# First relation pass of a graph kernel: TensorE picks the rows of every sixth tile from x on the chip, GpSimd gathers the others

## The chip, the cores and the metric

One core of a Trainium2 chip. The metric is the device time of one execution in microseconds (us). The engines: TensorE (PE; PEld is its weight load), VectorE (DVE), ScalarE (ACT), GpSimd (POOL) and SyncE (SP), which here only issues DMAs and passes semaphores on. In the profile "adj" is one large SBUF tensor that most buffers of the relation passes are carved from, so many tiles show under this name; "banks" is PSUM.

## The reference, cut to what matters

A stack of four graph layers over x (3125 nodes x 128) with 100,000 edges, sorted by destination; each layer is added to x and normalized. The last one is a two-layer relational convolution with 8 relations (128 to 256 to 128 features):

```python
def rgcn_layer(x, src, dst, etype, W, W_root, b, num_rels):
    h = jnp.einsum('ni,rio->rno', x, W)
    msg = h[etype, src]
    seg = dst * num_rels + etype
    sums = segment_sum(msg, seg, N * num_rels)
    cnt = segment_sum(ones, seg, N * num_rels)
    mean = sums / maximum(cnt, 1.0)[:, None]
    return mean.reshape(N, num_rels, do).sum(axis=1) + x @ W_root + b
h = relu(rgcn_layer(x, src, dst, etype, W1, root1, b1, 8))
out = rgcn_layer(h, src, dst, etype, W2, root2, b2, 8)
```

## The kernel before, in words

The edges are cut into T = 782 tiles of 128 edges, the nodes into 196 windows of 16. As the edges are sorted, a walk over JA = 977 steps meets each pair of tile and window that share an edge; most tiles take one step, some two. All of x, split in a high and a low f16 part (256 columns, "split"), also stands in HBM as table1.

At the start (until 66 us) the kernel works the walk out on the chip. VectorE turns the three edge lists into f16 pieces (line 1079 and after); ScalarE and VectorE make one-hot blocks "pick" that say which tile belongs to which step, in two batches (512 and 465 steps) of seven blocks; TensorE multiplies them with the pieces (L479, six matmuls per block); `expand` on VectorE (from L1131) turns the result into codes, windows and tile numbers, which SP stores in HBM. ScalarE begins with the queue of the parameter loads. Until 402 us the adjacency matrix is built from one-hot blocks (L1224 and L1232 on VectorE, L500 on TensorE, L856 on ScalarE), and until 890 us the first three layers run densely on TensorE.

Then come two relation passes with the matmuls of the two layers between (1874 to 2061 us). In a pass:

- GpSimd (`gather`, L766) fetches for each tile its 128 rows of 256 f16 from the table with one indirect DMA into one of NG = 16 buffers of `gath`; from the 17th on it first waits for `slot_free`.
- SP (`relay`, from L405) walks over the tiles in order: it waits until the last step of an old tile is scattered (L411, L412), frees its buffer (`slot_free`, L413 to L416), waits for the landing of tile t and raises `landed`. A buffer is freed eight tiles ahead of the landing that follows.
- VectorE (`relation_sums`, L1521) makes the one-hot block of step j + 4 (L1519, 128x128 f16), and adds the PSUM result of step j to the sums of its window (L1534, 128x129 f32).
- TensorE (`scatter`, L604) waits for the one-hot block, the tile and a free PSUM bank (six), and multiplies twice (L618: 129 and 128 columns). The buffer is chosen by a register, tile number modulo NG.
- ScalarE does nothing in a pass; in the first 83 steps it prepares weights, with pieces of this work on VectorE and TensorE (`between`).

Before the first pass GpSimd waits for the end of the dense layers, writes the ones column of `gath`, small constants and zeros over the sums (L753 to L757), then waits for table1.

## Time and profile before

| | us |
|---|---|
| median of 3 runs | 3111.7 (3109.05 to 3114.53) |
| profiled execution | 3108.86, span 3107.0 |
| walk and adjacency matrix | 0 to 402 |
| dense layers | 402 to 890 |
| first relation pass | 891 to 1874 |
| matmuls between the passes | 1874 to 2061 |
| second relation pass and end | 2062 to 3107 |

The page of the profile in 40 slices (each digit is the busy share in tenths, PEclk the granted clock of TensorE; the passes are the stretches with 7 on POOL):

```profile
PE   4777789989825444444444448964444444444447
DVE  6999949894156444444444445654444444444445
ACT  3555511111120000000000004520000000000003
POOL 0000000000157777777777771147777777777772
PEclk8888889999955555555555558975555555555558
```

A row of a timeline gives the start, the duration, engine, line, operation and tiles, and in brackets the idle time of the engine before it and what ended it. An engine may start an instruction before the duration of the last one has run out, so the distance of two starts is what an instruction costs in a full queue.

### The profile page before, as it was taken

The numbers are of one execution on the slowest core, as the hardware profiler recorded it, in microseconds if no ns is written. First come the engines' busy times: TensorE is split into PE (matmuls) and PEld (weight loads), VectorE is DVE, ScalarE is ACT, GpSimd is POOL, SyncE is SP. The second block draws the span as 40 slices with busy tenths as digits, with TensorE's granted clock in tenths as the row PEclk, the third lists the DMA queues.
The fourth block names the chain that finished last, engine by engine and source line by source line (L and its number), as shares of the span: only waits on it lengthen the run. The fifth ranks groups of instructions, "written<-read, shape, count | busy, mean of one in ns | idle before, by whom it ended". The sixth has DMA issues, their size and how long they took to land.

```text
span 3107.0 us, 50653 instructions
## 1 busy us (share of the span) xinstructions
PE 1742.9 (56%) x10220; PEld 961.0 (31%) x10220; DVE 1782.6 (57%) x6482; ACT 409.4 (13%) x868; POOL 1548.2 (50%) x1653
## 2 busy tenths in 40 slices
PE   4777789989825444444444448964444444444447
PEld 2333354544412222222222227742222222222227
DVE  6999949894156444444444445654444444444445
ACT  3555511111120000000000004520000000000003
POOL 0000000000157777777777771147777777777772
PEclk8888889999955555555555558975555555555558
DMA  2545510080112122222222221122222222222221
GB/s 63 128 117 117 124 42 1 1 263 2 48 49 54 53 54 54 54 54 53 54 53 54 54 54 52 76 71 53 53 54 54 54 53 53 54 53 54 53 54 29
DMA packets 174994, 191.72 MB, mean 62 GB/s; under 512 B 110509, under 2 KB 140990, under 8 KB 174723
## 3 DMA queue, kind: packets, MB, share of 16 engines
q0 software_dynamic: 50048, 102.60, 12.6%
q1 hardware_dynamic: 120774, 84.33, 9.8%
q8 instruction: 124, 2.03, 0.3%
q10 hardware_dynamic: 3900, 1.55, 0.2%
q14 instruction: 148, 1.20, 0.1%
HBM read 130.57 MB, written 38.14 MB: 54 GB/s over the span
## 4 chain that ended last, share of the span: by engine, by line
POOL 40%; PE 17%; DVE 15%; issue 15%; DMA 7%; SPq 3%; ACT 2%; ACTq 1%; DVEq 0%; POOLq 0%
POOL adj L766 40%; DVE hi_hot L1224 6%; DMA adj<-table,adj 6%; PE banks L528 4%; PE banks L543 4%; PE banks L662 3%; SPq L411 2%; DVE lo_hot L1232 2%; PE banks L674 2%; DVE deg_in L1392 2%; PE banks L714 2%; ACTq L848 1%; PE banks L647 1%; DVE stats L1280 1%; PE banks L506 1%
## 5 line engine op out<-in xcount | busy, mean ns | idle before, releaser
L766 POOL DMA_INDIRECT adj<-table,adj x1564 | 1478.6, 945 | 511.5 <-issue 454.4
L618 PE MATMUL banks<-adj 128*128 x3908 | 807.8, 286 | 1173.6 <-DVE adj L1519 778.1
L1534 DVE TENSOR_TENSOR adj<-adj,banks 128x129 f32 x1954 | 565.9, 290 | 1002.4 <-PE banks L618 919.5
L618 PEld LDWEIGHTS banks<-adj 128*128 128x128 f16 x3908 | 408.3, 105 | 1578.1 <-issue 1533.0
L1519 DVE TENSOR_SCALAR adj<-adj 128x128 f16<-128x128 f16 x1954 | 548.6, 281 | 1.5
L500 PE MATMUL banks<-hi_hot,lo_hot 128*128 128x400 f16 x977 | 248.1, 383 | 100.8 <-DVE hi_hot L1224 60.3
L1224 DVE TENSOR_SCALAR hi_hot<-iota,zT 128x400 f16<-128x400 f16 x977 | 250.9, 315 | 21.3 <-PE banks L500 21.2
L543 PE MATMUL banks<-adj,split 128*128 128x512 f16 (+1 forms) x1078 | 217.1, 359 | 0.0
L753 POOL MEMSET adj<- 128x32 f16 x1 | 0.1, 128 | 422.9 <-PE banks L543 422.9
L750 POOL PARTITION_ALL_REDUCE small<-small x1 | 0.4, 380 | 406.1 <-DVE small L1324 406.1
L500 PEld LDWEIGHTS banks<-hi_hot,lo_hot 128*128 128x128 f16 x977 | 114.9, 118 | 234.5 <-issue 172.7
L528 PE MATMUL banks<-adj,split 128*128 128x512 f16 (+1 forms) x672 | 138.9, 371 | 24.6 <-DVE adj L1419 13.6
L1046 ACT ACTIVATE adj<-adj 128x128 f32<-128x128 f32 x75 | 22.0, 387 | 987.0 <-DVE adj L1545 987.0
L1005 ACT ACTIVATE adj<-banks 128x512 f16<-128x512 f32 x50 | 26.9, 585 | 899.0 <-PE banks L647 899.0
L543 PEld LDWEIGHTS banks<-adj,split 128*128 128x128 f16 x1078 | 100.0, 99 | 108.2 <-issue 6.9
L856 ACT ACTIVATE adj<-banks 128x400 f16<-128x400 f32 x196 | 97.9, 501 | 158.9 <-PE banks L500 133.4
L1232 DVE TENSOR_TENSOR lo_hot<-iota,zT 128x512 f16<-128x512 f16 (+1 forms) x245 | 101.4, 415 | 0.0
L777 POOL MEMSET adj<- 128x1032 f32 x25 | 23.9, 957 | 154.5 <-PE banks L647 154.5
L528 PEld LDWEIGHTS banks<-adj,split 128*128 128x128 f16 x672 | 63.8, 101 | 98.9 <-issue 24.8
L860 ACT ACTIVATE banks<-banks 128x400 f32<-128x400 f32 x188 | 91.7, 488 | 6.0
L1392 DVE TENSOR_REDUCE deg_in<-adj 128x1 f32<-128x3200 f16 x25 | 85.1, 3475 | 0.0
L662 PE MATMUL banks<-adj,w1p 128*128 128x128 f16 x1350 | 84.2, 221 | 1.0 <-ACT h L1015 1.0
(241 smaller groups left out, 1280.7 us busy)
## 6 DMA issues: line engine op xcount, KB each, us to landing
adj<-table,adj POOLq DMA_INDIRECT x1564, 2.5
adj_copy<-adj SPq DMA_DIRECT2D x24, 800.0 KB, 3.9
adj<-adj_copy SPq DMA_DIRECT2D x6, 2176.0 KB, 15.8
table<-adj SPq DMA_DIRECT2D x25, 512.0 KB, 2.6
adj<-adj_copy SPq DMA_DIRECT2D x1, 3072.0 KB, 10.4
adj<-adj_copy SPq DMA_DIRECT2D x3, 1024.0 KB, 15.3
table<-split SPq DMA_DIRECT2D x6, 256.0 KB, 2.3
out_dram<-xres SPq DMA_DIRECT2D x6, 256.0 KB
```

Of the source, the lines that this page charges most:

```text
L500: e.matmul(banks[:, bass.ds(c, 1), 0:NC].rearrange("p o n -> p (o n)"), low, hi_hot[:, j % NHI, :], start=False, stop=True, skip_group_che ...
L528: m = e.matmul(sums_of(a, c), split[:, k, s, :], sources(a, k, c), start=(k == 0 and s == 0), stop=False)
L543: m = e.matmul(sums_of(a, c), split[:, k, s, :], sources(a, k, c), start=False, stop=(k == NB - 1 and s == 1))
L618: m = e.matmul(bank[j % NSUM][:, 0:b - a], hot[:, j % NHOT, :], edge[:, a:b], start=(q == 0), stop=(q == 1), skip_group_check=True)
L662: m = e.matmul(bank[3][:, o * P:o * P + P], w1p[:, wq, r, o * P:o * P + P], rowT[:, s, zq, r, :], start=(i == 0 and r == 0), stop=(i == 2 ...
L766: e.indirect_dma_start(gath[:, (t + 1) % NG, 0:2 * D], None, table, bass.IndirectOffsetOnAxis(ap=index[:, which, t:t + 1].bitcast(U32), ax ...
L856: e.activation(blocks[:, min(g + 1, LASTG), :, at * WA:(at + 1) * WA], v.rearrange("p (h n) -> p h n", n=WA), ACT.Copy).then_inc(evicted, 1)
L1224: e.tensor_scalar(hi_hot[:, j % NHI, :], iota[:, :], code[:, j:j + 1], None, ALU.is_equal).then_inc(high, 1)
L1232: e.tensor_tensor(lo_hot[:, g % NLO, :, 0:n], iota4[:, :, 0:n], lo[:, k:k + n].unsqueeze(1).broadcast_to([P, P, n]), ALU.is_equal).then_in ...
L1392: e.tensor_reduce(deg_in[:, b:b + 1], adj[:, b, :], AX.X, ALU.add).then_inc(in_degrees, 1)
L1519: e.tensor_scalar(hot[:, s, :], iota_r[:, :], code_r[:, j:j + 1], None, ALU.is_equal).then_inc(hot_set, 1)
L1534: e.tensor_tensor(a, a, bank[j % NSUM][:, 0:D + 1], ALU.add).then_inc(accumulated, 1)
```

## The change

In the first pass every sixth tile from tile 120 on (120, 126, ... 780: 111 tiles) is no longer gathered. Its rows are picked from `split`, which is now kept in SBUF through the pass (`place`, `hTp` and `h32` take its space afterwards). The source numbers of a picked tile, less 0, 640, ... 2560, were stored in HBM as f16 at the start (`scr_s`, by six GpSimd operations over 128x896 and one SP store). ScalarE's queue loads the five rows of a tile, broadcast to all partitions (`source_row`, 164 KB, two in flight). VectorE compares each row with a constant block of 5 x 128 node numbers (`select_hots`, one comparison of 128x640 f16 per step in five of six steps, steps 111 to 775), TensorE multiplies the five 128x128 blocks that come out with five blocks of `split` (`select_part`, 5 matmuls of 256 columns per step, steps 114 to 778), summing 25 in bank 6 or 7, and ScalarE copies the sum to one of NGX = 34 further buffers of `gath`. TensorE waits for that copy one step after the step without a part.

GpSimd gathers the other 671 tiles into NG = 18 buffers. SP raises `landed` for a picked tile without a wait. The buffer of a tile no longer follows from its number alone: buffer number times 1024 is added to the tile number in the walk. For this GpSimd makes a row of buffer numbers, stores it in HBM and loads it back by columns, VectorE copies it to a seventh piece before the others, each pick has a seventh matmul, and `expand` casts the word and masks the tile number out. In the second pass all tiles are gathered, into 18 buffers. The ones columns of the late buffers, which lie over w2, are written by VectorE at step 115; GpSimd's zeros over the sums move ahead of the ones block, and the ones block and the new constant wait for the last dense matmuls. The core of the diff:

```diff
+    KB = 5
+    PARTS = NB // KB
+    NG, NGX = 18, 34
+    by_pe = range(FROM, T, EVERY)
+    NPE = len(by_pe)
+    by_gather = [t for t in range(T) if t not in by_pe]
+    ROUND = EVERY * NGX
+    BUFS = FROM + -(-(TB * P - FROM) // ROUND) * ROUND
...
-        SUMS_OF = {0: [S_LO], 1: [S_HI, TYPE], 2: [D_LO, D_HI], 3: [TILE]}
+        SUMS_OF = {0: [S_LO], 1: [S_HI, TYPE], 2: [D_LO, D_HI], 3: [TILE, BUF]}
...
+            e.wait_ge(source_set, 1 + PARTS)
+            e.dma_start(scr_s, source16.rearrange("p b k e -> p b (k e)")).then_inc(source_out, 16)
...
+                block = None
                 for t in range(T):
                     u = t + LEAD - NG
-                    if u >= 0 and t + LEAD < T:
-                        if u % REGS == 0:
-                            n = min(REGS, T - NG - u)
-                            e.load(last_regs[0:n], last_row[:, u:u + n])
+                    if u >= 0 and u + NG in tiles_of(which):
+                        if u // REGS != block:
+                            block = u // REGS
+                            n = min(REGS, T - block * REGS)
+                            e.load(last_regs[0:n], last_row[:, block * REGS:block * REGS + n])
                         e.reg_alu(least, last_regs[u % REGS], 1, ALU.max)
                         if which:
                             e.reg_alu(least, least, JA, ALU.add)
                         e.wait_ge(scattered, least)
                         e.sem_inc(slot_free[which], 1)
-                    e.wait_ge(gathered[t % NG], 16 * (which * (-(-(T - t % NG) // NG)) + t // NG + 1))
+                    if t in tiles_of(which):
+                        e.wait_ge(gathered[t % NG], 16 * landings(which, t))
                     e.sem_inc(landed[which], 1)
...
+            def select_part(j):
+                i, q = divmod(j - FROM + EVERY, EVERY)
+                if q == 0 and 0 < i <= NPE:
+                    e.wait_ge(copied, i)
+                if q < PARTS and 0 <= i < NPE:
+                    e.wait_ge(selected, PARTS * i + q + 1)
+                    if q == 0 and i >= 2:
+                        e.wait_ge(copied, i - 1)
+                    for k in range(q * KB, (q + 1) * KB):
+                        m = e.matmul(bank[6 + i % 2][:, 0:2 * D], select[:, k, :], split[:, k, :, :].rearrange("p s d -> p (s d)"),
+                                     start=(k == 0), stop=(k == NB - 1), skip_group_check=True)
+                    m.then_inc(part_summed, 1)
+
             def scatter(which):
                 base = which * JA
                 for j in range(JA):
                     if j % WORDS == 0:
                         n = min(WORDS, JA - j)
                         e.load(tile_regs[0:n], tile_row[:, j:j + n])
-                    e.reg_alu(least, tile_regs[j % WORDS], 1, ALU.max)
+                    if which == 0:
+                        select_part(j)
+                    e.reg_alu(least, tile_regs[j % WORDS], (1 << BUF_LOG2) - 1, ALU.bitwise_and)
+                    e.reg_alu(least, least, 1, ALU.max)
                     e.wait_ge(hot_set, base + j + 1)
                     e.wait_ge(landed[which], least)
-                    c = e.snap(tile_regs[j % WORDS], min_val=1, max_val=T) % NG
+                    if which:
+                        c = e.snap(least, min_val=1, max_val=T) % NG
+                    else:
+                        word = e.snap(tile_regs[j % WORDS], min_val=1, max_val=((NG + NGX) << BUF_LOG2) - 1)
+                        c = word // (1 << BUF_LOG2)
...
+            e.iota(buf_row[:, :], pattern=[[0, BUFS // NG], [1 << BUF_LOG2, NG]], base=0, channel_multiplier=0,
+                   allow_small_or_imprecise_dtypes=True).then_inc(own_pool, 1)
+            e.wait_ge(own_pool, 1)
+            late = buf_row[:, FROM:BUFS].rearrange("a (c i s) -> a c i s", i=NGX, s=EVERY)[:, :, :, 0]
+            e.iota(late, pattern=[[0, (BUFS - FROM) // ROUND], [1 << BUF_LOG2, NGX]], base=NG << BUF_LOG2, channel_multiplier=0,
+                   allow_small_or_imprecise_dtypes=True).then_inc(own_pool, 1)
+            e.wait_ge(own_pool, 2)
+            e.dma_start(scr_b.rearrange("(a n) -> a n", a=1), buf_row[:, :]).then_inc(buffers_out, 16)
+            e.wait_ge(buffers_out, 16)
+            e.dma_start(buf_col[:, :], scr_b[0:TB * P].rearrange("(b q) -> q b", q=P),
+                        allow_slow_non_contiguous=True).then_inc(buffers_in, 16)
...
+            e.wait_ge(pieces_set, 1)
+            e.tensor_tensor(source[:, :, :], piece[:, S_LO, :, :], piece[:, S_HI, :, :], ALU.add).then_inc(source_set, 1)
+            e.wait_ge(source_set, 1)
+            for q in range(PARTS):
+                e.tensor_scalar(source16[:, :, q, :], source[:, :, :], -float(q * KB * P), None, ALU.add).then_inc(source_set, 1)
...
-            e.memset(gath[:, :, 2 * D:2 * D + 2], 1.0).then_inc(rel_set, 1)
+            e.memset(gath[:, 0:NEARLY, 2 * D:2 * D + 2], 1.0).then_inc(rel_set, 1)
             e.iota(iota_r[:, :], pattern=[[1, P]], base=0, channel_multiplier=0,
                    allow_small_or_imprecise_dtypes=True).then_inc(rel_set, 1)
+            e.memset(sums[:, :, :], 0.0).then_inc(sums_zero, 1)
+            e.wait_ge(mlp_sum, 2 * NCH)
             e.memset(ones_all[:, :], 1.0).then_inc(ones_set, 1)
-            e.memset(sums[:, :, :], 0.0).then_inc(sums_zero, 1)
+            e.iota(blocks5[:, :, :], pattern=[[P, KB], [0, P]], base=0, channel_multiplier=1,
+                   allow_small_or_imprecise_dtypes=True).then_inc(blocks5_set, 1)
...
-                for t in range(T):
-                    s = t % NG
+                for t in tiles_of(which):
                     if t >= NG:
-                        e.wait_ge(slot_free[which], t - NG + 1)
+                        e.wait_ge(slot_free[which], released[which].index(t) + 1)
                     e.indirect_dma_start(
-                        gath[:, (t + 1) % NG, 0:2 * D], None, table,
-                        bass.IndirectOffsetOnAxis(ap=index[:, which, t:t + 1].bitcast(U32), axis=0)).then_inc(gathered[s], 16)
+                        gath[:, (t + which) % NG, 0:2 * D], None, table,
+                        bass.IndirectOffsetOnAxis(ap=index[:, which, t:t + 1].bitcast(U32), axis=0)).then_inc(gathered[t % NG], 16)
 
             e.wait_ge(list_in, 80)
...
+            e.wait_ge(source_out, 16)
...
+            def source_row(i):
+                b, p = divmod(by_pe[i], P)
+                e.dma_start(source_rows[:, i % 2, :, :].rearrange("p k e -> p (k e)"),
+                            scr_s[p:p + 1, b, :].broadcast_to([P, PARTS * P])).then_inc(source_in[i % 2], 16)
+
+            for i in range(2):
+                source_row(i)
...
+            e.wait_ge(late_ones, 1)
+            for i in range(NPE):
+                e.wait_ge(part_summed, PARTS * (i + 1))
+                if i >= NGX:
+                    e.wait_ge(scattered, by_pe[i - NGX] + JA - T + 1)
+                e.activation(gath[:, NG + i % NGX, 0:2 * D], bank[6 + i % 2][:, 0:2 * D], ACT.Copy).then_inc(copied, 1)
+                if i + 2 < NPE:
+                    source_row(i + 2)
...
+            e.wait_ge(buffers_in, 16)
+            e.tensor_copy(piece[:, BUF, :, :], buf_col[:, :].unsqueeze(2).broadcast_to([P, TB, P])).then_inc(own_dve, 1)
...
-                e.scalar_tensor_tensor(out=WIN, in0=sets[3][:, 0:n], scalar=-1.0, in1=st, op0=ALU.mult,
-                                       op1=ALU.add).then_inc(own_dve, 1)
-                at_win = own.up()
+                e.tensor_copy(WORD, sets[3][:, 0:n]).then_inc(own_dve, 1)
+                at_word = own.up()
...
+                e.wait_ge(own_dve, at_word)
+                e.tensor_scalar(AT, WORD, (1 << BUF_LOG2) - 1, None, ALU.bitwise_and).then_inc(own_dve, 1)
...
+                e.wait_ge(own_dve, at_at)
+                e.tensor_tensor(WIN, st, AT, ALU.subtract).then_inc(own_dve, 1)
...
+            def select_hots(j):
+                i, q = divmod(j - FROM + EVERY + EVERY // 2, EVERY)
+                if q < PARTS and 0 <= i < NPE:
+                    if q == 0:
+                        e.wait_ge(source_in[i % 2], 16 * (i // 2 + 1))
+                    if i:
+                        e.wait_ge(part_summed, PARTS * (i - 1) + q + 1)
+                    e.tensor_tensor(select[:, q * KB:(q + 1) * KB, :],
+                                    source_rows[:, i % 2, q, :].unsqueeze(1).broadcast_to([P, KB, P]),
+                                    blocks5[:, :, :], ALU.is_equal).then_inc(selected, 1)
...
+                    if which == 0:
+                        select_hots(j)
...
+                elif t == 56 + RR + HB * RR:
+                    e.wait_ge(w_low, RR + HB * RR)
+                    e.memset(gath[:, NEARLY:NG + NGX, 2 * D:2 * D + 2], 1.0).then_inc(late_ones, 1)
```

## Rows read from the trace of the kernel before

**Rows 1.** The page: chain by engine; costliest group (busy, mean ns | idle before); DMA landing

```profile
POOL 40%; PE 17%; DVE 15%; issue 15%; DMA 7%; SPq 3%; ACT 2%; ACTq 1%; DVEq 0%; POOLq 0%
...
L766 POOL DMA_INDIRECT adj<-table,adj x1564 | 1478.6, 945 | 511.5 <-issue 454.4
...
adj<-table,adj POOLq DMA_INDIRECT x1564, 2.5
```

**Rows 2.** Busy time by stretch, the clock after the engines

```profile
core 0: us, PE busy (x) PEld busy (x) DVE busy (x) ACT busy (x) POOL busy (x), PEclk, DMA share, GB/s
66.00:400.00 334.00, 246.76 (x974) 114.31 (x972) 309.62 (x1209) 178.12 (x380) 0.00 (x0) 0.90 0.51 118
1200.00:1850.00 650.00, 268.40 (x1298) 135.46 (x1298) 315.12 (x1297) 0.00 (x0) 491.53 (x521) 0.50 0.20 54
1890.00:2050.00 160.00, 160.00 (x1833) 126.93 (x1832) 105.24 (x183) 82.77 (x183) 24.83 (x35) 1.00 0.18 74
```

**Rows 3.** Waits in 1200 to 1850: us in total, times, longest us

```profile
DVE adj L1534 <- PE banks L618: 304.6, 408, 2.8
...
POOL adj L766 <- issue: 152.7, 501, 0.3
...
POOL adj L766 <- SPq L416: 6.1, 20, 0.3
```

**Rows 4.** Timeline of GpSimd: first and last gather of the first pass

```profile
890.87 1.30 POOL L766 DMA_INDIRECT adj<-table,adj  x1 [23.24 <-DMA table<-split]
...
1867.03 0.94 POOL L766 DMA_INDIRECT adj<-table,adj  x1 [0.30 <-issue]
```

**Rows 5.** Timeline where work has piled up after a late landing

```profile
1504.40 0.29 DVE L1534 TENSOR_TENSOR adj<-adj,banks 128x129 f32 x1 [1.94 <-PE banks L618]
1504.60 0.25 DVE L1519 TENSOR_SCALAR adj<-adj 128x128 f16<-128x128 f16 x1
...
1504.72 0.41 PE L618 MATMUL banks<-adj 128*128 x2 [1.01 <-DVE adj L1534]
1504.91 0.29 DVE L1534 TENSOR_TENSOR adj<-adj,banks 128x129 f32 x1
...
1505.31 0.41 PE L618 MATMUL banks<-adj 128*128 x2 [0.18 <-DVE adj L1534]
```

**Rows 6.** Timelines of VectorE: f16 comparisons in the adjacency stage and before the pass

```profile
201.14 0.42 DVE L1232 TENSOR_TENSOR lo_hot<-iota,zT 128x512 f16<-128x512 f16 x1
...
201.48 1.02 DVE L1224 TENSOR_SCALAR hi_hot<-iota,zT 128x400 f16<-128x400 f16 x4
...
888.29 0.73 DVE L1519 TENSOR_SCALAR adj<-adj 128x128 f16<-128x128 f16 x4
```

**Rows 7.** TensorE in the chain: 112 matmuls of 512 columns, 12 of 465

```profile
420.85 24.27 PE banks L528 x112
...
44.45 4.96 PE banks L479 x12
```

**Rows 8.** Timelines: VectorE and GpSimd at the same time

```profile
898.74 0.94 POOL L766 DMA_INDIRECT adj<-table,adj  x1 [0.30 <-issue]
...
899.25 0.45 DVE L1519 TENSOR_SCALAR adj<-adj 128x128 f16<-128x128 f16 x1
...
2059.08 3.49 DVE L1692 TENSOR_TENSOR zT<-zT,xres 128x3200 f32<-128x3200 f32 x1
...
2061.67 1.77 POOL L766 DMA_INDIRECT adj<-table,adj  x1 [12.22 <-DMA table<-adj]
```

**Rows 9.** Timelines: start of the kernel, and GpSimd before the first pass

```profile
2.31 0.54 POOL L727 TENSOR_SCALAR adj<-ident 128x128 f16<-128x128 f32 x1
...
9.35 1.08 DVE L1079 CAST adj<-adj 128x896 f16<-128x896 f32 x1
...
21.84 1.33 ACT L828 ACTIVATE adj<-adj 128x512 f16<-128x512 f16 x2
...
846.03 21.60 POOL L757 MEMSET adj<- 128x25800 f32 x1
```

More of the change, by code:

```diff
@@ L19 @@
 GATES, ENDS = 8, 8
+EVERY, FROM = 6, 120
+BUF_LOG2 = 10
 WORDS = 8
@@ L777, in _ @@
                 e.memset(sums[:, nb * WPG:(nb + 1) * WPG, :], 0.0).then_inc(sums_zero, 1)
-            e.memset(place[:, :, :], 0.0).then_inc(own_pool, 1)
+            e.memset(place, 0.0).then_inc(own_pool, 1)
             half = ident[:, :]
```

71 lines of the change are left out of this document (52 added, 19 removed).

## The prediction

> **What bounds the kernel now.** First the shares: GpSimd is 40% of the chain that ended last, the largest part, and all but all its work is line 766, the gathers [rows 1]. Then the stretches: in 1200 to 1850 us GpSimd is busy 491.5 of 650 us, VectorE 315, TensorE 268 at a granted clock of 0.50, ScalarE nothing [rows 2]. The waits of the same stretch say that VectorE waits for TensorE, 304.6 us in 408 waits, while GpSimd has only 0.3 us ahead of each gather, 501 times "issue" and 20 times the release of a buffer by SP, and that is no longer than the others [rows 3]. So the relation passes go at GpSimd's own pace. The timeline prices that pace: the first gather of the first pass starts at 890.87, the last, the 782nd, at 1867.03, so (1867.03 - 890.87) / 781 = 1.250 us each, 0.944 of it busy and 0.30 between two [rows 1, 4]. The pass has 977 steps (one step is one tile with one window of 16 nodes), thus 1.00 us per step. What else a step needs is less: where work has piled up, VectorE does a step in 0.51 us (accumulate at 1504.40 and 1504.91) and TensorE in 0.59 us (1504.72, 1505.31) at half clock [rows 5].
>
> **What is removed.** 111 of 782 gathers (tiles 120, 126, ... 780) leave GpSimd: 111 x 1.250 = 139 us. The remaining 671 cost 671 x 1.250 = 839 us: the floor of the pass. A gather that is left out takes its wait, index read and DMA of 128 rows with it, all in this 1.250. That the gain is full needs VectorE, TensorE and the ring to follow at 0.8 x 1.250 x 5/6 = 0.83 us per step.
>
> **What VectorE gets.** In 665 steps (114 to 778, five of each six) one comparison of 128x640 f16 is added. Nearest row: the comparison of line 1232, also with a broadcast operand, 128x512 f16; the next instruction starts 0.34 us after it [rows 6]. By elements above some 0.07 fixed that is 0.40 us. A loaded step is accumulate 0.20 [rows 5], one-hot 0.16 to 0.31 (four in a row take 0.73 with 0.25 for the last, so 0.16 from start to start; 0.31 to the next accumulate, with register work that the new operation would now cover) [rows 5, 6], and 0.40: 0.76 to 0.91, and I take 0.86, with some 0.1 for waits at the port (below). With the sixth step at 0.51: (5 x 0.86 + 0.51) / 6 = 0.80 us per step, just under 0.83. If the comparison ran at half that pace, it would be 0.73. The comparison waits for its source row and for TensorE's part of the picked tile before, three steps back in TensorE's order; behind that wait stand all further accumulates, but TensorE is ahead of VectorE in any step: 0, unless TensorE is late itself (next).
>
> **What TensorE gets.** Five matmuls of 256 columns in each of these steps. 112 of 512 columns took 24.27 us at full clock, 0.217 each, so 0.11 us for 256; 12 of 465 at half clock took 4.96 us, 0.41 each, so 0.23 for 256 [rows 7]. Five: 0.54 or 1.14 us. The scatter's own step of 0.59 is 0.23 of loads and matmuls and 0.36 of waits and register work [rows 5], which its sequencer can do beneath queued matmuls, at best all of it. A loaded step is then 0.65 to 1.0 us at full clock and 1.37 to 1.73 at half; with the sixth step, 0.64 to 0.93 and 1.24 to 1.54. Here the granted clock decides. Now TensorE waits most of the time and has 0.50 (1.2 GHz). In 66 to 400 us, with 974 matmuls of 400 columns in 334 us (1.17 columns per ns), the clock was 0.90, thus four fifths of that time at 2.4 GHz; when it worked without a pause, 1890 to 2050, it was 1.00 [rows 2]. The changed stretch would have 25 x 256 + 6 x 257 = 7942 columns in six steps, 1.5 per ns at 0.87 us a step. At half clock it would not pause at all. I take four fifths at full clock: 0.8 / 0.80 + 0.2 / 1.3 = 1.15 steps per us, 0.87 us per step.
>
> **Ring and end.** The ring has 18 buffers, so gathers run at most 18 tiles ahead. When step 778 ends (about tile 624), tiles after 642 are still to fetch: 140 x 5/6 = 117 gathers, 146 us. The side of the steps is 114 x 1.00 + 665 x 0.87 + 146 + 4 for the last landing = 843 us, the gather side 839. As long as a step stays under about 0.87, gathers decide; each 0.01 us above adds 6.7 us.
>
> **The shared port.** First the rows. The one-hot of 899.25 fell into the gather of 898.74, took 0.45 instead of 0.25 us and ended with it, while those that start early in a gather take 0.25: GpSimd keeps VectorE off for a part of each gather. And the first gather of the second pass started at 2061.67 while an addition of two SBUF tensors, 2059.08 to 2062.57, ran; it took 1.77 instead of 0.94 us [rows 8]. That is the form of the new comparison: two SBUF inputs. In the first pass no such operation runs: the accumulate reads PSUM, the one-hot has one tensor. If a gather has to wait only where its start falls into a comparison, that is 5 x 0.33 of each 5.2 us, a chance of 0.32 with 0.17 us left on average: 0.05 us, for the some 445 gathers of the stretch 24 us. Bounds: 0 (the two fall into step and miss each other) and the whole 0.40 for each (178 us). I take 27 us. The Trainium skill (SBUF — State Buffer, Who interferes with whom) says that a VectorE instruction with two SBUF inputs contends with a GpSimd instruction that reads SBUF, and that the second to issue blocks until the first ends; it infers that descriptor generation needs only the write side. By the inference the loss would be 0 and the sum 27 us less; the trace's 1.77 us agrees with the block.
>
> **ScalarE, SP, DMA.** 111 copies of 128x256 (two of 128x512 take 1.33 [rows 9], so under 0.67 each) and 111 broadcast loads of 164 KB from HBM, queued behind them, lie on an engine that has nothing to do there [rows 2]; a load has some eight steps, 7 us, and a gather lands in 2.5 us [rows 1], so nothing of it shows. TensorE waits for the copy of a tile one free step after its last part; queued behind that wait is the scatter, with three steps in hand over VectorE: 0. The relay on SP passes over the picked tiles. The ones column of the late buffers is one small memset on VectorE at step 115, under 1 us. Before the pass GpSimd now does ones and block numbers after its 21.6 us of zeros, which end at 867.6, and has until the table is out at 890.87, 23 us of idle time [rows 4, 9]: 0. The second pass has two more buffers and one more register operation; its pace is GpSimd's: 0.
>
> **Start.** VectorE's copy of buffer numbers (1.08 like line 1079) waits for an HBM round trip on GpSimd's queue: two iotas after 4 us, some 1 to 2 us, a store of one row, 2.5 to land like a gather, and 896 pieces of 4 bytes, at most 896/128 x 0.94 = 6.6 us to issue, 2.5 to land: ready at 10 to 18 us, VectorE being ready for it at 10.4. It has some 4 us in hand, for the first pick waits for ScalarE, which has its queue of parameter loads and two copies ahead and begins at 21.84 [rows 1, 9]: 0 to 4, I take 1. A matmul more in each of 14 picks: 7 x 0.22 + 2 x 0.41 on the chain = 2.4. Per batch of 512 or 465 columns a cast and a mask more, at most 1.2 ns per column like line 1079 [rows 9]: 1.2 to 2.4, I take 1.9. GpSimd's six new passes over 128x896 can keep VectorE off its port (0.54 for 128x128 [rows 9], so up to 3 us each): 0 to 10, I take 1. The SP store of the picked rows' sources waits on them, ahead of the plan's stores, and ScalarE's first eviction at 66 waits for its landing: covered unless GpSimd is later than about 50. Behind GpSimd's own round trip stand its iotas and gates, which nobody needs before 60: 0. In all +6 (4 to 15).
>
> **Sum.** Against the profiled execution's 3108.9 us (span 3107.0; the median of three is 2.8 higher): gathers -139, port +27, steps that lag a little behind at low clock and at the change of pace +10, start +6, odds +2: -94, so 3015, and 3018 beside the median.
>
> **The rivals.**
> - Steps near 1.0 us per step: waits between engines or more time at half clock. 114 + 665 + 150 = 929 in place of 978, and +8 for start and odds: 3068. For it: VectorE and TensorE come within a few per cent of the pace. Against: 18 buffers smooth it.
> - TensorE stays at half clock, because it also waits for VectorE. 1.24 per step: 114 + 825 + 150 = 1089, +111 + 8: 3228; at 1.54 200 more. It decides from 1.06 us per step. Against: columns and clock of [rows 2].
> - The port, on the slower side: each gather of the stretch is held up by a whole comparison, 0.40 us: 839 + 178 = 1017, +39 + 8: 3156. It decides from 139 / 445 = 0.31 us per gather. The rule of the Trainium skill, SBUF — State Buffer, Who interferes with whom, would bring this about if a gather read SBUF throughout. Against: a one-hot early in a gather isn't delayed [rows 8].
> - The comparison runs at half pace, 0.73: (5 x 1.19 + 0.51) / 6 = 1.08 per step, 114 + 718 + 150 = 982, +4 + 8: 3121.
> - It doesn't do what it says: the time of the removed gathers returns as waits for landing or buffers: 3117.
>
> **How the numbers follow.** Forecast 0.53 (own range 2975 to 3045), steps near 1.0 0.24 (3045 to 3100), half clock 0.08, port 0.08, half pace 0.04, no effect 0.03. The lower end is the full 139 with a start of 4: 2974, and some less, 2970; the upper one takes in the second case: 3100. A measurement tells 0.2%, 6 us, from no change. Faster 0.80 (the first two and a little of the others), same 0.03, slower 0.17.
>
> **What would show it.** 671 gathers of the first pass, its last start near 1770; if start to start stays 1.25 in the stretch, the port is free, at 1.30 or more it isn't. The comparison at about 0.48 busy, next start 0.40 after. The clock of 1010 to 1600 near 0.9. GpSimd waiting for SP's release there would mean that the steps decide. The first eviction near 72 us. Wrong makes it a clock near 0.5 in the stretch, a comparison of 0.7, or gathers of 1.3 us busy.

## The result and the profile after

| | before | after |
|---|---|---|
| median, same chip | 3110.64 us (4 runs) | 3026.88 us (4 runs, 3025.28 to 3027.63) |
| profiled execution | 3108.86, span 3107.0 | 3026.34, span 3024.5 |
| first eviction of the walk's result | 66.22 | 86.51 |
| first relation pass, first to last gather start | 890.87 to 1867.03 | 913.15 to 1782.98 |
| second pass, first to last gather start | 2061.67 to 3038.28 | 1977.34 to 2955.32 |

The change makes the kernel 2.7% faster: the ratio is 0.9727 (95% interval 0.9715 to 0.9739), 84 us. The prediction said 3018 us with a range of 2970 to 3100, so it holds, and it promised 9 us too much. By the gathers' starts the first pass got 106.3 us shorter (976.2 to 869.8), while 22.3 us were lost ahead of it (first gather 890.87 to 913.15), and the second pass grew by 1.4 us (976.6 to 978.0).

The page of after: the 40 slices, the shares of the chain, and the lines that answer to [rows 1] and show the new work (after the bar: busy us, mean ns of one; then the idle us before them and what ended it).

```profile
PE   3677779998954578888886459944444444444447
DVE  5999977895344688888886556644444444444445
ACT  1555531111130000000000015500000000000003
POOL 3000000000037777777777751167777777777772
PEclk9888879999975699999997569955555555555558
...
POOL 34%; PE 20%; DVE 18%; issue 14%; DMA 10%; SPq 2%; ACT 1%; ACTq 1%; DVEq 0%; POOLq 0%
...
L850 POOL DMA_INDIRECT adj<-table,adj x1453 | 1407.4, 969 | 479.0 <-issue 399.0
...
L659 PE MATMUL banks<-split,zT 128*128 128x256 f16 x2775 | 397.1, 275 | 50.3 <-DVE zT L1638 35.0
...
L1638 DVE TENSOR_TENSOR zT<-zT,blocks 128x640 f16<-128x640 f16 x555 | 268.8, 484 | 0.0
...
L1095 ACT ACTIVATE adj<-banks 128x256 f16<-128x256 f32 x111 | 42.7, 385 | 579.0 <-PE banks L659 574.3
```

There are 1453 gathers where there were 1564, so 111 are gone. One is 0.969 us on average and was 0.945: this is the first trace of the port. In the slices of the stretch with picked tiles (15 to 21) VectorE is at 8 and TensorE at 7 or 8 where both were at 4, GpSimd still at 7, and the granted clock is 9 where it was 5. ScalarE's 111 copies take 0.385 us each, and it waits 574.3 us for TensorE ahead of them; TensorE in turn waits for them 0.3 us in the whole of 1050 to 1550.

By stretch (columns as in [rows 2]), with two more stretches of the pass and one of the second pass:

```profile
1010.00:1400.00 390.00, 308.88 (x2558) 216.64 (x2558) 314.98 (x1216) 25.96 (x68) 299.77 (x297) 0.96 0.32 80
1400.00:1590.00 190.00, 158.73 (x1363) 113.14 (x1364) 161.46 (x626) 14.03 (x37) 145.80 (x146) 1.00 0.35 84
1590.00:1775.00 185.00, 101.35 (x594) 56.65 (x592) 114.02 (x470) 2.69 (x7) 140.49 (x147) 0.60 0.22 58
2000.00:2900.00 900.00, 368.56 (x1800) 187.08 (x1800) 427.11 (x1798) 0.00 (x0) 680.75 (x720) 0.50 0.21 54
```

TensorE, now busy for 79 and 84% of the time, was granted 0.96 and then 1.00, that is 2.4 GHz nearly throughout; in the second pass, where little changed for it (one register operation more, 18 buffers in place of 16), it stayed at 0.50. VectorE is busy 81 to 85% of the changed stretch, and still GpSimd decides, as its waits in 1050 to 1550 show (compare [rows 3]):

```profile
DVE adj L1655 <- PE banks L684: 72.3, 133, 2.1
...
POOL adj L850 <- issue: 91.5, 300, 0.3
...
POOL adj L850 <- SPq L461: 24.4, 80, 0.3
```

No gather of this stretch, nor of the whole first pass, had more than 0.32 us ahead of it, whether "issue" or SP's release ended it. VectorE waits 72.3 us for TensorE in 500, where it waited 304.6 in 650. The steps have come close to the gathers' pace, but not past it.

### The profile page after: what moved, and what is told of

Read it like the earlier page. It is cut to its first block, busy times and chain, and to the rows that moved or that the text cites. A ratio compares the mean times of both kernels' runs of the same rounds, so it can differ in the third digit from the quotient of the medians.

```text
span 3024.5 us, 58937 instructions
## 1 busy us (share of the span) xinstructions
PE 1951.6 (65%) x13009; PEld 1166.5 (39%) x13009; DVE 1943.0 (64%) x7043; ACT 452.9 (15%) x979; POOL 1496.3 (49%) x1553
## 3 DMA queue, kind: packets, MB, share of 16 engines
q14 instruction: 153, 1.25, 0.1%
## 4 chain that ended last, share of the span: by engine, by line
POOL 34%; PE 20%; DVE 18%; issue 14%; DMA 10%; SPq 2%; ACT 1%; ACTq 1%; DVEq 0%; POOLq 0%
POOL adj L850 33%; DMA adj<-table,adj 9%; DVE hi_hot L1334 7%; PE banks L574 4%; PE banks L589 4%; PE banks L728 3%; DVE lo_hot L1342 2%; PE banks L740 2%; SPq L456 2%; DVE deg_in L1502 2%; PE banks L659 2%; PE banks L780 2%; PE banks L684 1%; PE banks L713 1%; ACTq L933 1%
## 5 line engine op out<-in xcount | busy, mean ns | idle before, releaser
L850 POOL DMA_INDIRECT adj<-table,adj x1453 | 1407.4, 969 | 479.0 <-issue 399.0
L684 PE MATMUL banks<-adj,hot 128*128 x3908 | 757.0, 265 | 815.1 <-DVE hot L1629 352.5
L684 PEld LDWEIGHTS banks<-adj,hot 128*128 128x128 f16 x3908 | 396.2, 101 | 1186.6 <-issue 1094.2
L1629 DVE TENSOR_SCALAR hot<-adj 128x128 f16<-128x128 f16 x1954 | 523.3, 268 | 1.5
L659 PE MATMUL banks<-split,zT 128*128 128x256 f16 x2775 | 397.1, 275 | 50.3 <-DVE zT L1638 35.0
L659 PEld LDWEIGHTS banks<-split,zT 128*128 128x128 f16 x2775 | 244.4, 98 | 84.4 <-issue 38.7
L1638 DVE TENSOR_TENSOR zT<-zT,blocks 128x640 f16<-128x640 f16 x555 | 268.8, 484 | 0.0
L1095 ACT ACTIVATE adj<-banks 128x256 f16<-128x256 f32 x111 | 42.7, 385 | 579.0 <-PE banks L659 574.3
## 6 DMA issues: line engine op xcount, KB each, us to landing
adj<-adj_copy SPq DMA_DIRECT2D x1, 3072.0 KB, 10.4
```

Source lines behind the costliest of these rows:

```text
L659: m = e.matmul(bank[6 + i % 2][:, 0:2 * D], select[:, k, :], split[:, k, :, :].rearrange("p s d -> p (s d)"), start=(k == 0), stop=(k == N ...
L684: m = e.matmul(bank[j % NSUM][:, 0:b - a], hot[:, j % NHOT, :], edge[:, a:b], start=(q == 0), stop=(q == 1), skip_group_check=True)
L850: e.indirect_dma_start(gath[:, (t + which) % NG, 0:2 * D], None, table, bass.IndirectOffsetOnAxis(ap=index[:, which, t:t + 1].bitcast(U32) ...
L1629: e.tensor_scalar(hot[:, s, :], iota_r[:, :], code_r[:, j:j + 1], None, ALU.is_equal).then_inc(hot_set, 1)
L1638: e.tensor_tensor(select[:, q * KB:(q + 1) * KB, :], source_rows[:, i % 2, q, :].unsqueeze(1).broadcast_to([P, KB, P]), blocks5[:, :, :], ...
```

## Experiments

The first four ran on the same chip as the kernels before and after, beside 11 further runs of the kernel before (median 3110.29).

### Is the pass shorter by the gathers, and is the start a price of its own?

**three_tiles** picks only tiles 768, 774 and 780 on TensorE. All that prepares for picking at the start stays.

```diff
-EVERY, FROM = 6, 120
+EVERY, FROM = 6, 768
```

> The changed kernel with the picked tiles starting at 768 in place of 120, so three tiles are picked and 779 gathered, while everything that the change adds at the start stays. Theory (the start costs 22 us whatever is picked, and the pass gains by the number of gathers): 3108.9 + 22 - 4 = 3127 us, first gather near 913 us as in the changed kernel, pass 1 at 974 us from first to last gather. Rival (part of the 22 us belongs to the picking of 111 tiles): under 3115 us and a first gather before 905.

Measured: 3129.38 us, ratio to before 1.0061 (1.0038 to 1.0084), so 0.6% slower than before; 3127 had been expected. Its gathers:

```profile
913.37 1.19 POOL L850 DMA_INDIRECT adj<-table,adj  x1 [24.22 <-DMA table<-split]
...
1886.48 0.95 POOL L850 DMA_INDIRECT adj<-table,adj  x1 [0.30 <-issue]
```

The first gather comes where it does in after (913.15), 22 us late, though next to nothing is picked; the pass of 779 gathers takes 973.1 us, 1.25 us each with 0.946 busy. So the loss at the start does not depend on the picking: the kernel is 19.1 us slower than before, and with the 3 x 1.25 us of its own missing gathers that makes 22.8 for the preparation.

### Do the comparisons slow the gathers down?

**no_compare** leaves out the comparisons of line 1638 after those for the first picked tile (the further picked tiles then use its blocks); all matmuls, copies and source rows stay.

```diff
                     if i:
                         e.wait_ge(part_summed, PARTS * (i - 1) + q + 1)
+                    if i:
+                        e.sem_inc(selected, 1)
+                        return
                     e.tensor_tensor(select[:, q * KB:(q + 1) * KB, :],
```

> The changed kernel without the comparisons of VectorE after the first picked tile: TensorE multiplies stale blocks, so 110 tiles get wrong rows; loads, matmuls and copies stay. Theory (the comparison with two SBUF inputs holds gathers up): gathers of the stretch fall from 1.01 to 0.945 us busy, from 1.32 to 1.25 from start to start, the pass from 870 to 843 us, in all near 3000 us. Rival (the row loads or the matmuls do it): gathers stay at 1.01 us and the time at 3026.

Measured: 2995.18 us (two runs, 2991.75 and 2998.62), 31.7 us below after; near 3000 had been expected. The first row here is the group of gathers in 1050 to 1550 of after, the second that of no_compare (busy, mean ns, idle before):

```profile
L850 POOL DMA_INDIRECT adj<-table,adj x380 | 384.9, 1013 | 115.8 <-issue 91.5 <-SPq L461 24.4
```

```profile
L850 POOL DMA_INDIRECT adj<-table,adj x401 | 379.2, 946 | 122.2 <-issue 105.1 <-SPq L461 17.1
```

Without the comparisons a gather takes 0.946 us as in before, with them 1.013; the 0.30 us between two are the same. The pass runs from these two gathers:

```profile
912.10 1.19 POOL L850 DMA_INDIRECT adj<-table,adj  x1 [24.35 <-DMA table<-split]
...
1750.50 0.94 POOL L850 DMA_INDIRECT adj<-table,adj  x1 [0.30 <-issue]
```

That is 838.4 us, the floor of 839 that the prediction worked out for 671 gathers. After needs 869.8, so the comparisons cost 31.4 us. 31.3 us of it is in the durations of the gathers (666.5 us in all against 635.2), 0.1 us in the time between them. The matmuls and the DMAs are the same in both, so of the change's new work it is the comparisons that gathers suffer from. This run alone doesn't say whether by the port or by VectorE's time.

### Is it the port, or VectorE's time?

Two kernels add to the kernel before what the change adds on VectorE, and nothing else: one comparison in 555 steps (five of each six), behind the step's accumulate, with a result that nobody reads (one memset at step 110 fills the inputs first). In **extra_two_sbuf** both inputs are in SBUF (128x640 f16), in **extra_one_sbuf** one is in PSUM (128x320 f32). The same lines stand in both, but for the comparison itself: each kernel has the one under its name (the comments are not in the kernels).

```diff
+            spin = zT[:, 0:4 * 320].rearrange("p (k n) -> p k n", n=320)
+            spin16 = zT[:, 0:4 * 320].bitcast(F16).rearrange("p (k n) -> p k n", n=640)
...
+                    if which == 0 and j == 110:
+                        e.memset(zT[:, 0:4 * 320], 1.0).then_inc(spin_set, 1)
...
+                    if which == 0 and 111 <= j < 777 and (j - 111) % 6 < 5:
+                        e.wait_ge(spin_set, spun.n)
+                        # extra_two_sbuf:
+                        e.tensor_tensor(spin16[:, 0, :], spin16[:, 1, :], spin16[:, 2, :], ALU.is_equal).then_inc(spin_set, 1)
+                        # extra_one_sbuf:
+                        e.tensor_tensor(spin[:, 0, :], bank[7][:, 0:320], spin[:, 2, :], ALU.is_equal).then_inc(spin_set, 1)
```

> The kernel before with one comparison of 128x640 f16 with two SBUF inputs added to steps 111 to 776 (five of six), whose result nobody reads. VectorE has 0.51 us of work in a 1.00 us step, so 0.40 more has room. Theory (port): the 532 gathers of that stretch take 1.01 to 1.02 us and start 1.31 to 1.32 us apart: 532 x 0.07 = 37 us, near 3147 us. Rival (row loads or matmuls slow the gathers, not VectorE): 0.945 us, 1.25 us and 3110 us.

> The kernel before with one comparison of 128x320 f32 in the same steps, one input from PSUM and one from SBUF, which takes VectorE as long as the 128x640 f16 one (about 0.40 us). Theory (only a second SBUF input takes the side that gathers need): gathers stay at 0.945 us, 3110 us. Rival (any VectorE work or any write of it slows them): as with two SBUF inputs, near 3147 us.

Measured: 3132.64 us for two SBUF inputs, ratio 1.0072 (1.0049 to 1.0095); 3109.95 us for one, ratio 0.9998 (0.9987 to 1.0009). The gathers of 1050 to 1600, first with two, then with one:

```profile
L767 POOL DMA_INDIRECT adj<-table,adj x428 | 420.9, 983 | 130.4 <-issue 115.2 <-SPq L417 15.2
```

```profile
L767 POOL DMA_INDIRECT adj<-table,adj x441 | 416.9, 945 | 134.4 <-issue 128.0 <-SPq L417 6.4
```

And a pair of rows of each timeline, a comparison and the gather that starts into it:

```profile
1299.70 0.48 DVE L1549 TENSOR_TENSOR zT<-zT 128x640 f16<-128x640 f16 x1
...
1299.89 1.11 POOL L767 DMA_INDIRECT adj<-table,adj  x1 [0.30 <-issue]
```

```profile
1305.68 0.48 DVE L1549 TENSOR_TENSOR zT<-banks,zT 128x320 f32<-128x320 f32 x1
...
1305.90 0.95 POOL L767 DMA_INDIRECT adj<-table,adj  x1 [0.30 <-SPq L417]
```

Both comparisons keep VectorE busy for 0.48 us. The gather that starts 0.19 us after the first one's start takes 1.11 us, the one 0.22 us after the second one's start 0.95. So it isn't VectorE's time, it is the second SBUF input. The two comparisons also differ in type, f16 against f32, and no run varies that alone. But two f32 inputs in SBUF hold a gather up as well: the first gather of the second pass, which starts into such an addition [rows 8], takes 1.75 to 1.77 us in every trace here, while the first gather of the first pass, with nothing on VectorE beside it, takes 1.19 to 1.30. And the f16 one-hots with one SBUF input, one in each step of the kernel before, leave its gathers at 0.945. The size was missed: 1.01 to 1.02 us busy, 1.31 from start to start and a time of 3147 had been expected, and the runs gave 0.983, 1.288 and 3132.6, about half to two thirds of it. Sorted by where the gather starts after the comparison's start, gathers of extra_two_sbuf take

| gather starts after the comparison's start | its duration |
|---|---|
| 0.05 to 0.10 us | 1.20 to 1.25 |
| 0.15 to 0.20 us | 1.10 to 1.15 |
| 0.20 to 0.25 us | 1.05 to 1.10 |
| 0.30 to 0.35 us | 0.95 to 1.00 |
| 0.35 us and later, into the comparison | 0.945 |

A delayed gather is longer by the rest of the comparison less some 0.125 us: this difference is 0.12 to 0.13 us for nine of ten of them, in extra_two_sbuf and in after. So a comparison that ends within 0.125 us of the gather's start costs nothing. Nor does one that begins 0.15 us or more into a gather: all but one of the 200 gathers of extra_two_sbuf into which one began 0.15 to 0.48 us after their start took 0.94 to 0.95 us. Of the 530 gathers of its stretch 151 started in the first 0.35 us of a comparison (0.28); in after it was 170 of 448 (0.38), and its mean is higher for that. How the two engines fall into step sets the size, and the expectation had taken the share of after for both. The comparison itself takes 0.48 us whatever the phase.

The Trainium skill (SBUF — State Buffer, Who interferes with whom) says that a VectorE instruction with two SBUF inputs contends with a GpSimd instruction that reads SBUF; the trace agrees (1.11 against 0.95). The page infers besides that the generation of a DMA's descriptors needs only the write side, and so isn't held up by such an instruction. Most of a gather fits that; its start doesn't run free, and whether it is the read of its 128 row numbers from SBUF that is held up there was not tried.

### What does the start consist of?

The trace of after, GpSimd's first 41 us (lines 817 and 820 work out the sources):

```profile
4.22 2.21 POOL L801 IOTA adj<- 1x936 f32 x1
...
7.18 0.79 POOL L808 DMA_DIRECT2D scr_buffer<-adj  x1 [0.31 <-POOL adj L805]
18.08 1.04 POOL L810 DMA_DIRECT2D adj<-scr_buffer  x1 [10.12 <-DMA scr_buffer<-adj]
...
25.83 1.92 POOL L817 TENSOR_TENSOR adj<-adj 128x896 f32<-128x896 f16 x1 [5.04 <-DVEq L1199]
27.84 12.92 POOL L820 TENSOR_SCALAR adj<-adj 128x896 f16<-128x896 f32 x5
```

and VectorE's:

```profile
22.27 1.09 DVE L1184 CAST adj<-adj 128x896 f16<-128x896 f32 x1 [12.19 <-DMA adj<-scr_buffer]
...
26.03 1.74 DVE L1202 TENSOR_TENSOR adj<-adj 128x7 f32<-128x7 int32 x1
```

The same operation in both_again (below), which has nothing on GpSimd at that time:

```profile
14.13 0.17 DVE L1215 TENSOR_TENSOR adj<-adj 128x7 f32<-128x7 int32 x1
```

The store of 3.7 KB landed 10.6 us after its issue, the load behind it 4.2 us after its own, and VectorE stood still for 12.19 us, until 22.27; 12.19 us earlier it had been ready for this cast, at 10.1 (the prediction had 10.4). Then GpSimd's passes over the sources took 1.92 + 12.92 us, and VectorE's operation on 128x7 numbers beside the first of them took 1.74 us where it takes 0.17 alone. Two causes, then: the round trip, and the source passes, which hold VectorE up. Four kernels take them away.

**buffers_on_chip** computes the buffer numbers on VectorE, with 15 small operations on 128x7 numbers, and has no round trip:

```diff
-            e.dma_start(scr_b.rearrange("(a n) -> a n", a=1), buf_row[:, :]).then_inc(buffers_out, 16)
-            e.wait_ge(buffers_out, 16)
-            e.dma_start(buf_col[:, :], scr_b[0:TB * P].rearrange("(b q) -> q b", q=P),
-                        allow_slow_non_contiguous=True).then_inc(buffers_in, 16)
...
+            dve(e.scalar_tensor_tensor(out=R18, in0=X[0], scalar=-18.0, in1=tile, op0=ALU.mult, op1=ALU.add))
...
+            e.wait_ge(own_dve, dve(e.tensor_tensor(buf_col[:, :], LB, R18, ALU.add)))
```

> The changed kernel with the buffer numbers worked out by 15 small VectorE operations (128x7 and 128x14) in the time in which it waits for the edge lists, without GpSimd's row, its store and its load. Theory (the round trip keeps VectorE waiting from 10.1 to 22.3 us, of which ScalarE's queue had covered 4 or less): the first eviction comes 10 to 12 us earlier, at 75 to 77 us, in all 3015 us. Rival (the extra matmuls and expand operations are what counts): no more than 3 us.

**sources_by_act** lets ScalarE write the five tables of sources, from the integers that were loaded, and takes GpSimd's six passes out:

```diff
-            e.tensor_tensor(source[:, :, :], piece[:, S_LO, :, :], piece[:, S_HI, :, :], ALU.add).then_inc(source_set, 1)
-            e.wait_ge(source_set, 1)
-            for q in range(PARTS):
-                e.tensor_scalar(source16[:, :, q, :], source[:, :, :], -float(q * KB * P), None, ALU.add).then_inc(source_set, 1)
...
+            for q in range(PARTS):
+                e.activation(source16[:, :, q, :], tab_i[:, 0, :, :], ACT.Copy, bias=-float(q * KB * P)).then_inc(source_set, 1)
```

> The changed kernel with the five blocks of source numbers made by ScalarE from the edge list after its picks (5 x 0.8 us in its idle time) in place of GpSimd's six operations (14.9 us busy). Theory (GpSimd holds the shared port, so VectorE's operations between 26 and 40 us take longer, 1.74 in place of 0.17 for a small one): 5 us less, 3021 us. Rival (hidden): within 2 us of 3026.

**both_and_later** is the two together, and it issues the first two source-row loads behind the wait for the table:

```diff
+            e.wait_ge(l3_in, 16 * (3 + HB))
+            e.wait_ge(table1_out, 16 * NQ)
             for i in range(2):
                 source_row(i)
-            e.wait_ge(l3_in, 16 * (3 + HB))
-            e.wait_ge(table1_out, 16 * NQ)
```

> Both of these, and the first two row loads of ScalarE's queue moved behind the landing of the table (they were issued 0.4 us before the last store of the table, which landed 3.5 us after its issue in place of 2.1). Theory: 12 + 5 + 1.4, near 3008 us, first gather near 895 us, first eviction near 70. Rival (extra matmuls and expand operations): 3020 or more.

**x_after_buffers** only makes the load of x, issued by SP, wait for the round trip: does x hold the store up?

```diff
+            e.wait_ge(buffers_in, 16)
             e.dma_start(xres[:, 0:FULL, :], io["x"][0:FULL * P, :].rearrange("(b p) d -> p b d", p=P)).then_inc(x_in, 16)
```

> The changed kernel with the load of x (1.6 MB) on SP's queue held back until the buffer numbers have come back. Theory (the store of 3.7 KB took 10.6 us to land because it stood behind the load of x and the parameter rows in the same 16 DMA engines): it lands in under 5 us, VectorE resumes before 17 us, some 5 to 7 us less in all: 3020 us. Rival (a store from GpSimd's queue is slow by itself at the start): still about 10 us, 3026 us.

These four ran on another chip, on which the kernel before needs 3559.18 us, because its relation passes are slower there (below). Times are thus compared inside a chip; the start hardly differs between chips (first eviction of the unchanged after: 86.51 on the first, 86.04 on the third). One trace is one execution: three traces with the same start (before, extra_one_sbuf, extra_two_sbuf) have their first eviction at 66.22, 67.40 and 68.69 and the first gather at 890.87, 891.75 and 890.64. So a difference under some 2.5 us says nothing at the first eviction, nor one under some 1 us at the first gather.

| kernel | us | first eviction | first gather |
|---|---|---|---|
| buffers_on_chip | 3487.42 | 74.3 | 899.4 |
| sources_by_act | 3491.42 | 82.0 | 908.7 |
| both_and_later | 3480.97 | 70.2 | 898.0 |
| x_after_buffers | 3497.36 | 83.5 | 908.3 |

The first evictions expected were 75 to 77 and near 70 for buffers_on_chip and both_and_later. The four runs of both_and_later lie 20 us apart (3475.32 to 3494.88), so its time carries little. After itself was not among them, so three were repeated beside it on a third chip (before there 3599.28).

> The changed kernel itself, beside which the next three are read on one chip (the chip of the four runs before needs 3559 us for the kernel before, 14% more, all of it in the relation passes). Theory: first eviction at 86.5, first gather at 913 us.

> Buffer numbers worked out by VectorE, sources by ScalarE, first row loads behind the table: what is left of the start's cost is 14 matmuls and two operations per batch, 4.3 us by the prediction. Theory: first eviction at 70 to 71 us, first gather 15 to 17 us earlier than in the changed kernel, 15 to 17 us less in all (0.5%). Rival (the earlier start is lost again in the dense layers, which wait for a load or for the clock): under 8 us.

> Only the buffer numbers worked out by VectorE. Theory: 12 us less than the changed kernel, first eviction near 74.5 us.

> The load of x held back until the buffer numbers are back. Theory (the round trip stands behind x and the parameter rows): at the first try the first eviction came at 83.5 us, so 3 us earlier; the same again, and 3 us less in all. Rival (no effect of x): 86.5 us.

| kernel | us | ratio to before | first eviction | first gather |
|---|---|---|---|---|
| after_again | 3518.08 | 0.9769 (0.9752 to 0.9785) | 86.04 | 911.25 |
| both_again | 3506.60 | 0.9746 (0.9729 to 0.9762) | 70.97 | 896.80 |
| buffers_again | 3510.16 | 0.9753 | 75.66 | 902.2 |
| x_after_again | 3521.99 | 0.9786 | 83.75 | 911.0 |

The first evictions, which carry the verdict, of after_again, buffers_again and both_again:

```profile
86.04 0.51 ACT L941 ACTIVATE adj<-banks 128x400 f16<-128x400 f32 x1 [7.71 <-PE banks L546]
```

```profile
75.66 0.50 ACT L932 ACTIVATE adj<-banks 128x400 f16<-128x400 f32 x1 [7.70 <-PE banks L548]
```

```profile
70.97 0.51 ACT L930 ACTIVATE adj<-banks 128x400 f16<-128x400 f32 x1 [7.71 <-PE banks L548]
```

The round trip was worth 10.4 us (86.04 to 75.66), the source passes another 4.7 (75.66 to 70.97, and 5.4 at the first gather with the row loads below; alone, beside a round trip that still stands, 82.0 against some 86). Together 15.1 of the 20 us. What is left, 70.97 against 66.22 before, is 4.8 us, and 5 to 6 us at the first gather (896.80 against 890.64 to 891.75): it fits the picks' extra matmul and the wider expansion of the lists, priced at 2.4 + 1.9 = 4.3, but no run takes these two away. The times follow in part: both_again is 11.5 us below after_again where 15 to 17 had been expected, buffers_again 7.9 where 12 had been. That the intervals of the ratios overlap makes this more a matter of the traces' 14.4 us at the first gather than of the times.

The other 2 us of the 22.3 came between the first eviction and the first gather, and most of them are the first two row loads. These are issued while the last store of the table is under way. Its landing (us from issue), in before and then in after:

```profile
table<-split SPq DMA_DIRECT2D x1, 64.0 KB, 1.6
```

```profile
table<-split SPq DMA_DIRECT2D x1, 64.0 KB, 3.0
```

In all nine traces with the loads ahead of the wait it takes 2.7 to 3.0 us, buffers_on_chip (2.8) and sources_by_act (2.8) among them, which have the other two edits one by one; in both_and_later and both_again, which move the loads behind the wait, it is 1.6 again. So the loads cost 1.1 to 1.4 us.

x_after_buffers missed: its store landed in 8.2 us, where under 5 had been expected, and in sources_by_act on the same chip, with x loaded as usual, it took 8.3. Over all traces it takes 8.3 to 11.0 us with the load of x ahead and 7.6 and 8.2 without. In x_after_again the first eviction came 2.3 us earlier than in after_again, near the 3 us expected but within the spread; the first gather came only 0.2 us earlier (911.01 against 911.25) and the time is 3.9 us longer, not 3 us shorter. So x is at most a small part of the store's slowness, and holding it back gains nothing; whether the rest is the other parameter loads or the queue itself was not tried and stays open.

The fastest version measured on its chip is thus both_again, 3506.6 against 3599.3 before, clear of noise, and against 3518.1 after, which is not. It was not run on the first chip.

## Why the prediction was right, point by point

| step of the prediction | predicted | measured |
|---|---|---|
| 111 gathers removed, at 1.250 | -139 | -137.8 (976.2 to 838.4, no_compare) |
| port | +27 (0 to 178) | +31.4 (838.4 to 869.8) |
| steps behind at low clock, change of pace | +10 | about 0 (no gather of the pass waited over 0.32) |
| start | +6 (4 to 15) | +22.3 (890.87 to 913.15) |
| second pass, middle, end | +2 | +1.7 (1.4, -0.2, 0.5) |
| sum of the span | -94 | -82.5 |

**What bounds it.** Right: GpSimd's own pace, before and after. The first working of the pass, 671 x 1.250 = 839, is what no_compare shows to 0.6 us.

**VectorE's step.** A loaded step was put at 0.76 to 0.91, taken at 0.86. Where work had piled up, after measured this:

```profile
1309.10 0.28 DVE L1655 TENSOR_TENSOR adj<-adj,banks 128x129 f32 x1
...
1309.46 0.48 DVE L1638 TENSOR_TENSOR zT<-zT,blocks 128x640 f16<-128x640 f16 x1
1309.87 0.28 DVE L1655 TENSOR_TENSOR adj<-adj,banks 128x129 f32 x1
```

From accumulate to accumulate it is 0.77 us, the lower end. The comparison is busy 0.48 us with the next start 0.41 later, as scaled from [rows 6] (0.40); the rival of the half pace (0.73) falls by this row.

**TensorE's step and the clock.** Five matmuls were put at 0.54 us at full clock:

```profile
1306.07 0.71 PE L659 MATMUL banks<-split,zT 128*128 128x256 f16 x5
1306.61 0.31 PE L684 MATMUL banks<-adj,hot 128*128 x2
```

1306.61 - 1306.07 = 0.54. The clock was taken at full for four fifths of the stretch, as in 66 to 400 us [rows 2]; it was granted at 0.96 and 1.00. So neither the rival with TensorE at half clock nor the one with steps near 1.0 us came about: a step of 1050 to 1550 took 500 / 566 = 0.883 us, and that is the gathers' pace: 1.318 us from start to start x 0.80 tiles per step x 5/6 of them gathered = 0.88. That GpSimd sets it is shown by its longest wait of 0.3 us, and the same sum fits no_compare: 1.250 x 0.80 x 5/6 = 0.83, measured 500 / 597 = 0.838.

**Steps that lag.** This term was a hedge without a row, and nothing came of it: with both engines under the gathers' pace there was no lag to pay. That the ring's 18 buffers took up the change of pace fits this; no run has fewer. The last gather started at 1782.98 instead of near 1770, and the later start (16 us more than taken) explains all of these 13 us.

**The port.** The mechanism that was taken from the gather of 2061.67 [rows 8] is the one that the two extra kernels show, and 0.05 to 0.06 us for each of 445 gathers became 0.07 for each of 448. The row was a weaker witness than it was taken for: the first gather of the first pass takes 1.30 us too, with nothing beside it [rows 4], so up to 0.36 of the 0.83 us above 0.94 may be a first gather's own. And there was luck in the size: the prediction counted 0.33 us of each comparison as the time in which a start is delayed. Measured, the comparison lasts 0.48 us and some 220 of the 448 gathers start inside one, but the first 0.35 us alone delay them (170), by the rest less 0.125. The slower rival (0.40 for each) would have needed the whole comparison to stand against each gather; a gather is held only if it starts inside one:

```profile
1304.69 0.48 DVE L1638 TENSOR_TENSOR zT<-zT,blocks 128x640 f16<-128x640 f16 x1
1304.75 1.24 POOL L850 DMA_INDIRECT adj<-table,adj  x1 [0.31 <-issue]
```

This one starts 0.06 us into a comparison and takes 1.24 us.

**The start.** This is the step that failed: +22.3 in place of +6, beyond its own bound of 15. It was mis-sized in three terms. The store's landing was taken as that of a gather in the middle of the kernel, 2.5 us [rows 1]; in the first 20 us it took 10.6, and the load 4.2. So the numbers were ready at 22.27 instead of 10 to 18, and the round trip, taken at 1 us, cost 10.4: of the 4 us in hand only 1 was there (VectorE waited 11.47 us in after_again). GpSimd's passes over the sources were allowed 0 to 10 us of obstruction and taken at 1; they cost 4.7. The bound of 15 was also set too low by the prediction's own terms, whose upper ends add up to 4 + 2.4 + 2.4 + 10 = 19. And the first two source rows, priced at nothing because ScalarE has nothing to do, stand ahead of its wait for the table. In after that wait ends here, ahead of the first instruction behind it:

```profile
912.36 2.12 ACT L1077 ACTIVATE zT<-adj 128x2304 f32<-128x2304 f32 x1 [3.50 <-DMA table<-split]
```

It was 2.08 us before. The last store of the table, for which it waits, landed 3.0 us after its issue instead of 1.6, and the traces above put these 1.1 to 1.4 us down to the two loads. What held, as far as the traces tell, was the picks and the expansion (4.8, give or take the spread of 2.5, against 4.3).

So the total was right partly by two errors of opposite sign: the lag of +10 that did not come and the start that cost 16 more.

## What to carry to other kernels

A price that is read from the middle of a kernel doesn't hold in its first 20 us: a small round trip through HBM there cost 10 us on the path, and a few numbers that can be computed on the engine that needs them are better computed there (10.4 us at the first eviction, 9 at the first gather). When work is moved onto VectorE beside a GpSimd that gathers, count the SBUF inputs: 0.48 us of comparison with one input in PSUM cost nothing, with two in SBUF 555 of them lengthened the pass by 20 us. And an engine's clock is to be judged by what it will do after the change, not by what it was granted before.

## What the runs showed of the hardware that was not expected

**The hold is at the gather's start only.** A gather that starts inside a comparison with two SBUF inputs takes up to 1.25 us, one that starts 0.15 us or more before it 0.945, though the two then overlap. One-hots of one input are the other way round: those that start some 0.45 to 0.70 us into a gather end with it, 0.49 us instead of 0.25, and those earlier don't [rows 8].

**Chips differ in the scatter loop.** On the second and third chip the same kernels need 14 to 16% more. Between the traces of after and after_again lie 499 us, of which 473 are between the first and the last gathers of the two passes (869.8 to 1096.8, and 978.0 to 1223.7) and the others behind them; the start is 2 us shorter. Waits of the second pass, 2400 to 2900 us, in after and then in after_again:

```profile
PE banks L684 <- issue: 57.9, 192, 0.4
```

```profile
PE banks L684 <- issue: 263.3, 295, 3.8
...
POOL adj L850 <- SPq L461: 120.8, 96, 3.1
```

TensorE has gaps of up to 3.8 us in which nothing in the profile holds it, and GpSimd then waits for buffers, up to 3.1 us: there the steps decide. What the gaps are was not found. The first pass is no different there; in 1100 to 1700 of after_again:

```profile
POOL adj L850 <- SPq L461: 178.1, 164, 3.1
```

The change brings 81 us there too (3599.28 to 3518.08), against 84 on the first chip, but not as this document explains it: with GpSimd waiting for buffers, a gather less is not 1.25 us less. The kernel before was not profiled on these chips, so what the 81 us are made of is open.
